# Slot tables of a top-2 expert layer: 24 broadcast comparisons replaced by 128 per-column ones

## What is computed

```python
def _L0_ffn_ref(x, gate_w, w1, b1, w2, b2):
    xt = x.reshape(-1, 256)
    probs = softmax(xt @ gate_w.T)                 # 8 experts
    top_w, top_i = top_k(probs, 2)
    top_w = top_w / (top_w.sum(-1) + 1e-09)
    h = gelu(einsum('td,ndh->tnh', xt, w1) + b1)   # hidden width 1024
    out_all = einsum('tnh,nhd->tnd', h, w2) + b2
    sel = take_along_axis(out_all, top_i[:, :, None], axis=1)
    return (sel * top_w[:, :, None]).sum(axis=1)
x = x + _L0_ffn_ref(layernorm(x), ...)
```

## Time and profile before

| | us |
|---|---|
| median of 3 runs | 1970.18 |
| lowest and highest | 1963.88, 1970.23 |
| the profiled execution | 1965.34 |
| its span | 1963.2 |
| TensorE busy | 1697.4 (86%) |
| VectorE busy | 1224.3 (62%) |
| ScalarE busy | 1115.6 (57%) |
| GpSimd busy | 617.0 (31%) |

### The profile page before, as it was taken

One profiled execution on the slowest core, in us unless ns is written; L12 is line 12 of the kernel. 1 busy time (PEld: TensorE's weight loads), 2 busy tenths in 40 slices (PEclk: granted clock), 3 DMA queues, 4 the chain that ended last, 5 costly groups with the idle time before them and its releaser, 6 DMA issues. The chain is left out here.

```text
span 1963.2 us, 40701 instructions
## 1 busy us (share of the span) xinstructions
PE 1697.4 (86%) x13407; PEld 1387.9 (71%) x13412; DVE 1224.3 (62%) x4212; ACT 1115.6 (57%) x2552; POOL 617.0 (31%) x783
## 2 busy tenths in 40 slices
PE   6677777769999999999987999999996999999963
PEld 5545555557788888889976877777774777777742
DVE  6689999968210011111117899999954988888756
ACT  2289999942222222222326656666643888888855
POOL 3433332331211111100114666666632122222217
PEclk9889999989999999999989999999997999999985
DMA  3100001025765555547944000000002111111002
GB/s 118 47 26 18 27 18 27 2 86 189 253 204 170 194 180 183 191 164 240 333 154 167 22 22 22 19 15 22 22 1 67 40 34 34 34 34 34 2 1 86
DMA packets 111695, 171.96 MB, mean 88 GB/s; under 512 B 6832, under 2 KB 86576, under 8 KB 110864
## 3 DMA queue, kind: packets, MB, share of 16 engines
q1 hardware_dynamic: 95248, 142.55, 22.0%
q0 software_dynamic: 6480, 17.70, 3.0%
q10 hardware_dynamic: 9776, 9.31, 1.4%
HBM read 143.45 MB, written 26.08 MB: 86 GB/s over the span
## 5 line engine op out<-in xcount | busy, mean ns | idle before, releaser
L1886 ACT ACTIVATE moe_hT<-moe_p_h,lane_a 128x256 f32<-128x256 f32 (+1 forms) x344 | 131.2, 433 | 370.6 <-PE moe_p_h L1828 370.5
L1828 PE MATMUL moe_p_h<-moe_gT,moe_w 128*128 128x256 f32 (+1 forms) x1376 | 255.7, 344 | 0.8 <-issue 0.8
L1838 PE MATMUL moe_p_y<-moe_w,moe_hT 128*128 128x256 f32 x1136 | 252.3, 379 | 0.0
L1828 PEld LDWEIGHTS moe_p_h<-moe_gT,moe_w 128*128 128x128 f32 x1376 | 227.2, 191 | 25.5 <-issue 1.0
L1336 ACT ACTIVATE xb_pr<-xb_sc,xb_nmax 128x256 f32<-128x256 f32 x512 | 221.2, 502 | 39.3 <-DVE xb_nmax L1393 39.1
L1838 PEld LDWEIGHTS moe_p_y<-moe_w,moe_hT 128*128 128x128 f32 x1136 | 212.5, 190 | 27.1
L1393 DVE CUSTOM_DVE_ANT_0 xb_sc<-xb_p_s,xb_neg 128x256 f32<-128x256 f32 x512 | 187.1, 420 | 54.6 <-PE xb_p_s L1202 53.2
L837 ACT ACTIVATE xa_pr<-xa_sc,xa_nmax 128x256 f32<-128x256 f32 (+1 forms) x512 | 204.2, 453 | 17.0 <-DVE xa_nmax L917 16.2
L1718 POOL DMA_INDIRECT moe_gx<-moe_tokens,moe_source_i x71 | 67.3, 948 | 456.2 <-PE moe_p_t L1815 400.3
L2031 DVE TENSOR_TENSOR moe_gy<-moe_p_y,lane_a 128x256 f32<-128x256 f32 x71 | 27.5, 421 | 229.1 <-PE moe_p_y L1838 229.1
L2006 DVE COPY moe_gT<-moe_p_t 128x512 f32<-128x512 f32 (+1 forms) x43 | 25.7, 598 | 231.9 <-PE moe_p_t L1815 226.1
(11 more groups left out here) (343 smaller groups left out, 3432.3 us busy)
## 6 DMA issues: line engine op xcount, KB each, us to landing
moe_w<-in_L_ffn_w_dram SPq DMA_DIRECT2D x86, 1024.0 KB
moe_rows_out<-moe_gy ACTq DMA_DIRECT2D x28, 256.0 KB
xb_kv<-moe_w SPq DMA_DIRECT2D x18, 256.0 KB, 2.4
X<-in_x_dram SPq DMA_DIRECT2D x4, 1024.0 KB, 8.3
xa_ctx<-in_ctx_turned_dram SPq DMA_DIRECT2D x16, 256.0 KB, 2.9
moe_tokens<-moe_XN_s SPq DMA_DIRECT2D x16, 256.0 KB, 2.2
xb_k_in<-xb_kv SPq DMA_DIRECT2D x16, 256.0 KB
xb_v_in<-xb_kv SPq DMA_DIRECT2D x16, 256.0 KB
```

Of the source, the lines that this page charges most:

```text
L1828: last = pe.matmul(p_h[n % 3][:, k * width:(k + 1) * width], w1[:, r, ic, (2 * n + k) * P:(2 * n + k + 1) * P], gT[:, r % 2, ic, 0:width], ...
L1838: last = pe.matmul(p_y[:, t * D:(t + 1) * D], hT[:, hc, t * P:(t + 1) * P], w2[:, r, hc, :], start=(hc == 0), stop=(hc == HC - 1))
L1886: last = act.activation(hT[:, 2 * n + k, 0:width], p_h[n % 3][:, k * width:(k + 1) * width], ACT.Gelu, bias=b1[:, bass.ds(e * HC + 2 * n + ...
```

## The change

Each table column is now made by itself, in one instruction that compares the ramp with a number read per partition. For `at_blk` a second operation of the same instruction multiplies by the token number, also read per partition. The numbers are read from the 32-bit `blk`, `row` and `token`, so the three 16-bit copies and their casts go. The group's signal to TensorE now comes from its last `at_row`.

```diff
-        token_h = ph.sb("token_h", [P, NT], F16)
-        blk_h = ph.sb("blk_h", [P, 2 * NT], F16)
-        row_h = ph.sb("row_h", [P, 2 * NT], F16)
...
             chain.done(pool.tensor_copy(ramp_h[:, :], ramp[:, :]))
-            chain.wait()
-            chain.done(pool.tensor_copy(token_h[:, :], token[:, :]))
             chain.wait()
             pool.sem_inc(s_["set_up"], 1)
...
             step(dve.scalar_tensor_tensor(flat(row[:, :, :]), flat(blk[:, :, :]), -float(P), flat(place[:, :, :]), ALU.mult, ALU.add))
-            chain.done(dve.tensor_copy(blk_h[:, :], flat(blk[:, :, :])))
-            step(dve.tensor_copy(row_h[:, :], flat(row[:, :, :])))
             for g in range(2 * NT // 8):
-                own = slice(8 * g, 8 * g + 8)
-                of = slice(8 * g % NT, 8 * g % NT + 8)
                 if g >= 4:
                     dve.wait_ge(s_["hot_read"], g - 3)
-                chain.done(dve.tensor_tensor(at_blk[:, g % 4, :, :], ramp_h[:, 0:NBLK].unsqueeze(1).broadcast_to([P, 8, NBLK]),
-                                             blk_h[:, own].unsqueeze(2).broadcast_to([P, 8, NBLK]), ALU.is_equal))
-                chain.done(dve.tensor_tensor(at_row[:, g % 4, :, :], ramp_h[:, :].unsqueeze(1).broadcast_to([P, 8, P]),
-                                             row_h[:, own].unsqueeze(2).broadcast_to([P, 8, P]), ALU.is_equal))
-                chain.wait()
-                dve.tensor_tensor(at_blk[:, g % 4, :, :], at_blk[:, g % 4, :, :],
-                                  token_h[:, of].unsqueeze(2).broadcast_to([P, 8, NBLK]), ALU.mult).then_inc(s_["hot"], 1)
+                for n in range(8):
+                    k, t = divmod(8 * g + n, NT)
+                    dve.tensor_scalar(at_blk[:, g % 4, n, :], ramp_h[:, 0:NBLK], blk[:, k, t:t + 1], token[:, t:t + 1], ALU.is_equal, ALU.mult)
+                    last = dve.tensor_scalar(at_row[:, g % 4, n, :], ramp_h[:, :], row[:, k, t:t + 1], None, ALU.is_equal)
+                last.then_inc(s_["hot"], 1)
```

## The result

The change makes the kernel 0.18% slower: the ratio of the times on record is 1.0018, 95% interval 1.0011 to 1.0026, from 20 executions each. That is 3.5 us, 2.2 to 5.1, where 2.4 was forecast. The two medians by themselves, 1967.37 us before and 1969.60 us with the change, lie 2.2 us apart, and the profiled execution took a span of 1964.4 us against 1963.2: the size of the effect is known to a us or two from the times, and closer only from the profile.

A forecast was written before the change was run, and what follows sets the result against it. The bound was taken to be one chain from VectorE's slot tables through the gather to TensorE's expert matmuls. Tables ready at 502.15 against 499.72 us gave +2.4, so 1970.18 became 1972.6 us, range 1965.5 to 1979.

The forecast's parts named there:

- The chain: VectorE's slot tables through gather to the first expert matmul: a later tables' end moves all behind it one for one.
- The price of an instruction: VectorE's table instructions: 0.21 us for 71 columns, 0.155 for 128, so 2.92 us a group against 2.58.
- a straight line through two rows: VectorE's 128-column instruction with one read, priced from the 256- and 512-column rows: 0.15 us.
- a sum of parts: VectorE's 128-column instruction, priced as fixed part, columns and one read number: 0.16 us.
- The time as such: Whole kernel: profiled execution 1965.34 to 1967.7 us, plus the 4.8 by which the median lay above it, 1972.6.
- The casts: VectorE ahead of the table loop: two casts removed, the loop starting 0.33 us sooner, at 478.66.
- POOL's root: POOL's root after the removed cast and wait: gain costed at nothing, 0.3 us or so if its cover were gone.
- Waiting again from the fourth group on: TensorE in the tables: after 4.02, about 2.7 and 2.08 us groups it waits, its work hidden behind VectorE's 2.92.
- Absolute places: Profile after: source tokens near 502.7 us and the first expert matmul near 509.5.
- Rival 1: VectorE's scalar reads overlap, group 1.48 us, TensorE's 2.08 the bound: 1965.3 to 1968 us; chance 0.20.
- Rival 2: VectorE's table instructions run at 1.06 ns a column, steps 0.26 us: +12.9 us, 1983.1; chance 0.09.
- The rule beside it: VectorE's tables by 58 cycles plus columns over the mode's factor, reads unpriced: 94 + 79 ns a column, half the old time.

The follow-up runs named there:

- e3: The change with a second read number (1.0) and a multiplication in the 128-column instruction, result the same; ratio to before 1.0033, +6.5 us.
- e1: The change with constants in place of the numbers read per partition, routing left out, every gather index the same token; ratio to before 1.0000.
- e7: e1 with made-up gather indices that lie apart, routing still left out; ratio to before 0.9993, -1.4 us.
- e12: e10 with the multiplication waiting only for the comparison of at_blk, not for that of at_row; ratio to before 0.9982, -3.5 us.
- e2: The change with the token number in the 71-column instruction replaced by the constant 2.0, one read instead of two; ratio to before 1.0005, +1.0 us.
- e6: Before with both tables laid out with the 8 columns innermost and the ramp copied 8 times, still 24 instructions; ratio to before 1.0022, +4.3 us.
- e10: Before with columns innermost in the 128-wide table only and two context projections moved ahead of the groups; ratio to before 0.9979, -4.1 us.

## Why the prediction was right

The forecast of +2.4 us and the mechanism behind it held, step by step.

- *The chain.* The tables' length moves the end one for one: +2.79 and +2.78 in the change, +6.7 and +6.6 in e3.
- *The price of an instruction.* 0.21 us for the fused one, as summed. 0.16 instead of 0.155 for the other, so a column is 0.371 instead of 0.365 and a group 2.97 instead of 2.92: 64 x 0.006 = 0.4 us, the whole difference between the 2.4 of the sum and the 2.8 of the trace. The term that was undersized is that of the 128-column instruction, taken between a straight line through two rows (0.15) and a sum of parts (0.16); the sum of parts was right. The measured 3.5 us has both 2.4 and 2.8 in its interval.
- *The time as such.* 1972.6 us was forecast and 1969.60 measured. Most of these 3.0 us are not the change: the forecast started from the median of three executions, 1970.18, and over 20 the median of before is 1967.37. The same 20 executions give the ratio to within 0.08%, far finer than the 0.5% that the prediction allowed a measurement.
- *The casts.* 0.33 us before; they are gone. POOL's root was costed at nothing, and against POOL's first cast it starts as before (2.80 us behind it, 2.81 before).
- *TensorE.* Waiting again from the fourth group on, as forecast, and the granted clock held through the waits of 0.71 us (1.00 from 488.9 to 501 us). The first two groups were forecast at 4.02 and about 2.7 us and took 2.96 and 2.97: the first one began at full clock. Both hide behind VectorE, so the sum did not suffer.
- *Absolute places.* The source tokens were forecast near 502.7 and the first expert matmuls near 509.5; they came at 501.29 and 508.16. Against `row`, which came 1.76 us sooner, they are where they should be. I gave times of the clock for what is a distance; that part was badly put.
- *Rival 1 (reads overlap).* Out, by e1 and e3. Its floor was right: without reads the chain up to the gather came 3.3 and 4.9 us sooner, the latter with eight groups of 2.08. (Its group of 1.48 us is a slip, 8 x 0.18 is 1.44; e1 has 1.52, and nothing hangs on it.) Only 2.3 of the 4.9 us reached the last expert matmuls in e7, with made-up indices; in e12, with the real ones, all 5.0 did.
- *Rival 2 (no fast mode).* Out: the comparison runs at 0.01 us for 57 columns in e2, an odd width and 32-bit numbers included.
- *The rule beside it.* By the formula of the Trainium skill (VectorE: DVE Perf Modes, The TRN2 errata) a column would have cost 0.17 us, as an estimate. Where no number is read it comes within 0.02 us of the run (0.19 us a column in e1); of the change's 0.37 it misses 0.20, most of it the three reads.

## What to carry to other kernels

Count an instruction as fixed part, columns and numbers read: fusing a multiplication into a comparison by turning two wide broadcast instructions into eight narrow ones saved a pass over 568 columns here, paid eight fixed parts and sixteen reads for it, and lost 0.2 us a group. Before making one engine's piece shorter, ask who then sets the pace and how the other engine reads the new layout: e6 cut VectorE's group from 2.58 to 1.46 us and lost, and the shorter tables came through only where the streamed table kept its layout and two of TensorE's projections moved into its wait (e10). Compare runs by distances between two instructions of the same run, when the layers ahead wander by more than the effect.

## What the runs showed of the hardware that I had not expected

- A number read per partition costs VectorE 0.05 to 0.06 us each, also in a row of 128 like instructions, where I had left one chance in five that it would be hidden.
- A two-source 16-bit instruction runs at about half the price per column if both operands move in the innermost direction (568 columns 0.37 us from start to start), and at the full price if one stands still there (0.67).
- TensorE reading 16-bit tables with 16 bytes between elements: eight matmuls of 71 columns 0.64 us with the weights so, 1.19 with the streamed table so, 1.22 with both, 0.44 with neither.
- A gather whose 128 indices name one row was turned 8.3 us after its issue (e1), against 6.1 with made-up indices that lie apart (e7) and 4.9 with the real ones.
